# A transformer layer with attention and experts on one core: scores and maxima as pairs of 64-partition tiles, with a new order of TensorE's work

## The chip, the cores and the metric

The kernel runs on one core of a Trainium2 chip. The metric is the device time of one execution in microseconds (us), lower is better. TensorE's granted clock was 0.993 of full speed on average over the profiled execution.

## The reference

The input `x` holds 1024 tokens (a 32 x 32 image) of 384 channels. The layer is attention with decomposed relative positions, then a mixture of experts, each with a normalisation ahead and a residual behind:

```python
qkv = x @ w_qkv + b_qkv                      # 12 heads of 32 channels
attn = einsum('bnd,bmd->bnm', q * scale, k)  # 1024 x 1024 for each head
attn = attn + rel_h[..., :, None] + rel_w[..., None, :]   # rows r and columns w of the key's place
attn = softmax(attn); out = attn @ v
x = x + out @ w_proj + b_proj
# experts: top 2 of 8, 40 slots for each expert and group of 128 tokens, relu(t @ wi) @ wo, combined by the gates
```

`rel_h[q, r]` is the product of query q with a table row that depends on its own image row and on r; `rel_w[q, w]` likewise for image columns. All operands are 32-bit floats; the kernel splits the factors of its large products into a high and a low part of a rounded type (`fp32r`), and adds the products of the parts.

## The kernel before

The program is one list of instructions for each engine, written by hand, and semaphores are the only order between the lists. TensorE (PE) runs its list strictly in the order written. The stages are: load and normalise; project q and k (`qk`); relative terms (`rel_products`, `rel_turn`); values (`value_tile`, eight tiles of tokens, with max products between them); twelve heads of attention (`head`); projection; routing; experts. The change touches everything from the relative terms to the end of the heads.

For a head, one operand of 128 partitions holds all that a score needs. Query side `qst[b]` has 32 partitions of q, 32 of the low part of q (part 0) or of a row with the negated maximum (part 1), 32 of `rel_h` and 32 of `rel_w`. Key side `kst[b]` has k, k again or ones, and 64 constant rows (one-hot of the key's image row and column) that pick the relative terms. So a tile of 128 keys against 512 queries takes two matmuls of 128 x 128 x 512, and a score tile of 128 keys x 1024 queries takes four (`scores`, L597). `max_scores` (L584) makes the scores of 128 queries against 512 keys once more with one matmul, so that the largest of a row can be taken; there are 16 of them for a head (piece p). VectorE (DVE) takes the maximum of each piece (`reduce_max`, L1188), of all pieces (`whole_max`, L1192), TensorE turns the 128 x 8 result (`turn_max`, L589), DVE negates it (`negate_max`, L1198), and a small transfer puts it into `qst` (`max_row`, L340). The maxima run one head ahead: in `head(h)` TensorE makes pieces 5 to 15 for head h+1 and 0 to 4 for head h+2. Pieces use three PSUM banks in turn, so piece p waits until piece p-3 has been reduced.

ScalarE (ACT) takes the exponential of a score tile (L979) into one of six slots `prob`. GpSimd (POOL) adds seven of a head's eight tiles into `acc` (`add_probs`, L419 and L423), so that TensorE needs only the eighth tile and `acc` for the sum of a row. `values` multiplies each tile with the head's values as four column tiles of 32 (`quarters`, L606), two `prob` tiles for each i; with i = 3 it also does the sums (`ones` with `prob` and with `acc`). `pv_mm` then lets POOL begin the adds of the next head. `turn_output` (L630) turns the output and DVE normalises it.

The SyncE queue (SP) issues the transfers. `gather_head(h+2)` waits for the last score of head h-1 and then copies 32-partition strips inside SBUF into `qst` and `kst` in six transfers (1280 KB); it is needed by piece 0 of head h+2. Three buffers b = h mod 3 are used.

Of the kernel before, what the change touches and what calls it, by code (L numbers as in the profile page):

```python
# [5 lines left out]
ALU = mybir.AluOpType  # L6
# [13 lines left out]
def metaformer_layer(nc, x, w_qkv, b_qkv, w_proj, b_proj, rel_pos_h, rel_pos_w, w_router, wi, wo,  # L20
# [69 lines left out]
    attn = place("attn", [P, NT, D], F32, u1)  # L90
# [15 lines left out]
    rel = [new(n, [P, 2, DC, T], F32R) for n in ("relh", "relw")]  # L106
# [3 lines left out]
    onehot = place("onehot", [P, T], F32, v0 + 8 * BANK)  # L110

    q0, q1 = room(16 * T), room(16 * T)
    qst = [place(f"qst{b}", [P, 2, T], F32R, at_b) for b, at_b in enumerate((q0, q1, x0))]
    kst = [place(f"kst{b}", [P, 2, T], F32R, at_b + 8 * T) for b, at_b in enumerate((q0, q1, x0))]
# [9 lines left out]
    rhalf = new("rhalf", [P, NT, 2])  # L124
# [40 lines left out]
    with ctx:  # L165
# [8 lines left out]
        def wait(eng, s, value):  # L174
# [17 lines left out]
        xb_ready, k_rows, rows_set = sem("xb_ready"), sem("k_rows"), sem("rows_set")  # L192
# [4 lines left out]
        rel_products_mm, rel_copied, rel_mm, rel_act, rel_dve = (  # L197
            sem(n) for n in ("rel_products_mm", "rel_copied", "rel_mm", "rel_act", "rel_dve"))

        heads_in = [sem(f"heads_in{b}") for b in range(3)]  # L200
        vh_ready, max_mm, max_red, max_whole, max_turned, mneg_ready, mrow_in = (
            sem(n) for n in ("vh_ready", "max_mm", "max_red", "max_whole", "max_turned", "mneg_ready", "mrow_in"))
# [30 lines left out]
        HEAD_IN = 16 * 6  # L233
# [5 lines left out]
        REL = [(kind, c, half) for c in range(DC) for kind in range(2) for half in range(2)]  # L239
# [4 lines left out]
        PAIRS_T = NT // 2  # L244
        ADDED = 7
# [36 lines left out]

        def rel_views(part, n):


            kind, c, half = REL[n]
            b, w = bank(2 + n % 2), SIDE // 2
            if kind == 0:
                return rel[0][:, part, c, half * BANK:(half + 1) * BANK], b
            return (rel[1][:, part, c, :].rearrange("p (r w) -> p r w", w=SIDE)[:, :, half * w:(half + 1) * w],  # L290
                    b.rearrange("p (r w) -> p r w", w=w))
# [3 lines left out]
        def _(sp):  # L295
# [10 lines left out]
            sp.dma_start(onehot[2 * SIDE:4 * SIDE, :], onehot_c).then_inc(onehot_in, 16)  # L306
# [4 lines left out]
            def gather_head(h):  # L311
# [9 lines left out]
                if h in (1, 2):  # L321
                    sp.wait_ge(rows_set, 2)
                    sp.wait_ge(k_rows, 1)
                    for const, part in ((slice(2 * HD, 4 * HD), slice(0, 2)), (slice(HD, 2 * HD), slice(1, 2))):
                        sp.dma_start(kst[h][const, part, :].bitcast(F32), kst[0][const, part, :].bitcast(F32)).then_inc(rows_in[h - 1], 16)
                if h > 2:
                    sp.wait_ge(s_mm, 8 * (h - 2))
                both = [HD, 2, T]
# [6 lines left out]
                for dst, src in parts:  # L335
                    sp.dma_start(dst.bitcast(F32), src.bitcast(F32)).then_inc(heads_in[b], 16)  # L336

            def max_row(h):
                sp.wait_ge(mneg_ready, h + 1)
                sp.dma_start(qst[h % 3][HD:HD + 1, 1, :].rearrange("o (t q) -> o t q", q=P).bitcast(F32),  # L340
                             mneg[:, :].bitcast(F32)).then_inc(mrow_in, 16)
# [3 lines left out]
            gather_head(1)  # L345
            for h in range(NH):
                max_row(h)
                if h + 2 < NH:
                    gather_head(h + 2)
                if h == NH - 2:  # L350
                    sp.wait_ge(s_mm, 8 * (NH - 2))
                    sp.dma_start(wpj[:, :, :], w_proj.rearrange("(c p) n -> p c n", p=P)).then_inc(wpj_in, 16)
# [25 lines left out]
        def _(pool):  # L378
            nc.gpsimd.memset(ones[:, :], 1.0).then_inc(ones_set, 1)

            for i in range(2 * DC + 1):
# [8 lines left out]
                if i == 0:  # L390
# [4 lines left out]
            pool.wait_ge(onehot_in, 16)  # L395


            nc.gpsimd.memset(qst[0][HD:2 * HD, 1, :].bitcast(F32), 0.0).then_inc(rows_set, 1)
            nc.gpsimd.memset(kst[0][HD:2 * HD, 1, :].bitcast(F32), 1.0).then_inc(rows_set, 1)
            pool.wait_ge(rows_set, 2)  # L400
            nc.gpsimd.tensor_copy(kst[0][2 * SIDE:4 * SIDE, :, :],
                                  onehot[2 * SIDE:4 * SIDE, :].unsqueeze(1).broadcast_to([2 * SIDE, 2, T])).then_inc(k_rows, 1)
            pool.wait_ge(k_rows, 1)
            pool.wait_ge(ones_set, 1)
            pool.wait_ge(proj_mm, 4 * DC)
            nc.gpsimd.memset(qst[1][HD:2 * HD, 1, :].bitcast(F32), 0.0).then_inc(rows_set, 1)
            pool.wait_ge(rows_set, 3)
            pool.wait_ge(v_dve, NT)

            def head_values(h, b):  # L410

                wait(pool, pv_mm, PAIRS_T * (h - 2))
                nc.gpsimd.tensor_copy(vh[b][:, :, :], vt[:, :, bass.ts(h, HD)]).then_inc(vh_ready, 1)

            def add_probs(h, j, added=ADDED):

                pool.wait_ge(exp_done, NT * h + 2)
                wait(pool, pv_mm, PAIRS_T * h)
# [1031 lines left out]
```

## Time and profile before

| | us |
|---|---|
| median of 3 runs | 602.74 (600.71 to 602.84) |
| the profiled execution, its own time | 603.15 |
| its span, first to last instruction | 601.3 |
| relative terms 2nd and 3rd chunk, about 47.1 to 62.6 | 15.5 |
| value tiles, 62.6 to 77.4 | 14.8 |
| heads 0 to 11, 77.4 to about 276 | 199 |
| head 0, first exponential to that of head 1, 78.98 to 94.00 | 15.0 |
| one head in the middle | 16.52 |

The profile gives busy time by engine and by line. TensorE's busy time counts overlapping matmuls once. A matmul's duration is longer than the distance to the next, since they are pipelined: what a matmul costs is the distance between two starts. PEld are weight loads, which run under the matmul before.

### The profile page before, as it was taken

The numbers are of one execution on the slowest core, as the hardware profiler recorded it, in microseconds if no ns is written. First come the engines' busy times: TensorE is split into PE (matmuls) and PEld (weight loads), VectorE is DVE, ScalarE is ACT, GpSimd is POOL, SyncE is SP. The second block draws the span as 40 slices with busy tenths as digits, with TensorE's granted clock in tenths as the row PEclk, the third lists the DMA queues.
The fourth block names the chain that finished last, engine by engine and source line by source line (L and its number), as shares of the span: only waits on it lengthen the run. The fifth ranks groups of instructions, "written<-read, shape, count | busy, mean of one in ns | idle before, by whom it ended". The sixth has DMA issues, their size and how long they took to land.

```text
span 601.3 us, 11451 instructions
## 1 busy us (share of the span) xinstructions
PE 587.1 (98%) x4459; PEld 511.5 (85%) x4459; DVE 383.0 (64%) x643; ACT 295.2 (49%) x411; POOL 196.7 (33%) x115
## 2 busy tenths in 40 slices
PE   7999999999999999999989999999999999999996
PEld 7787977766677766668988999999999999999994
DVE  6646777777677776624888865554567555367525
ACT  4555245555555555563646444454545444455523
POOL 2300068889899888897000000000000000000000
PEclk9999999999999999999889999999999999999999
DMA  8046064444333334103412444443443434543202
GB/s 264 21 87 134 1 132 89 89 90 87 71 68 67 69 75 87 40 3 106 157 41 81 157 158 158 155 146 130 133 147 105 150 141 159 158 157 97 101 1 105
DMA packets 38615, 63.40 MB, mean 105 GB/s; under 512 B 3912, under 2 KB 34478, under 8 KB 38446
## 3 DMA queue, kind: packets, MB, share of 16 engines
q1 hardware_dynamic: 38574, 62.83, 37.0%
q8 instruction: 29, 0.48, 0.3%
q14 instruction: 12, 0.10, 0.0%
HBM read 44.16 MB, written 1.57 MB: 76 GB/s over the span
## 4 chain that ended last, share of the span: by engine, by line
PE 91%; DVE 3%; DMA 2%; ACT 1%; SPq 1%; issue 1%; DVEq 0%
PE ps L822 21%; PE ps L838 21%; PE ps L597 13%; PE ps L606 9%; PE ps L501 8%; PE ps L584 7%; PE ps L533 2%; PE ps L756 1%; PE ps L793 1%; PE ps L544 1%; PE ps L849 1%; PE ps L768 1%; SPq L336 1%; DMA kst<-kp 1%; PE ps L630 1%
## 5 line engine op out<-in xcount | busy, mean ns | idle before, releaser
L1188 DVE TENSOR_REDUCE rhalf<-ps 128x1 f32<-128x512 f32 x192 | 130.8, 690 | 33.6 <-PE ps L584 33.3
L423 POOL TENSOR_TENSOR acc<-acc,prob 128x1024 f32<-128x1024 f32 x58 | 139.7, 2408 | 8.7 <-ACT prob L979 4.0
L979 ACT ACTIVATE prob<-ps 128x1024 f32<-128x1024 f32 x96 | 98.1, 1028 | 80.7 <-PE ps L597 80.3
L597 PE MATMUL ps<-qst,kst 128*128 128x512 f32 x384 | 115.3, 396 | 0.5 <-DMA qst<-mneg 0.3
L451 POOL CAST dpc<-dpt 120x1024 fp32r<-120x1024 f32 (+1 forms) x3 | 3.1, 1042 | 274.8 <-PE ps L858 216.6
L822 PE MATMUL ps<-xeh,wih 128*128 128x320 f32 x288 | 89.6, 311 | 1.0 <-ACT xeh L1043 1.0
L838 PE MATMUL ps<-hh,woh 128*128 128x320 f32 x288 | 89.2, 310 | 0.0
L838 PE MATMUL ps<-hh,wol 128*128 128x320 f32 x288 | 89.0, 309 | 0.0
L822 PE MATMUL ps<-xeh,wil 128*128 128x320 f32 x288 | 89.0, 309 | 0.0
L838 PE MATMUL ps<-hl,woh 128*128 128x320 f32 x288 | 89.0, 309 | 0.0
L822 PE MATMUL ps<-xel,wih 128*128 128x320 f32 x288 | 89.0, 309 | 0.0
L597 PEld LDWEIGHTS ps<-qst,kst 128*128 128x128 f32 x384 | 70.1, 188 | 17.5 <-ACT prob L979 2.1
L584 PE MATMUL ps<-kst,qst 128*128 128x512 f32 x192 | 77.0, 407 | 1.4 <-DMA kst<-kp 0.8
L1276 DVE TENSOR_TENSOR wol<-raw_o,woh 128x1152 fp32r<-128x1152 f32 x32 | 43.4, 1357 | 50.8 <-ACT woh L1016 50.8
L1047 ACT ACTIVATE hh<-ps 128x320 fp32r<-128x320 f32 x96 | 41.8, 439 | 55.7 <-PE ps L822 55.1
L1016 ACT ACTIVATE woh<-raw_o 128x1152 fp32r<-128x1152 f32 x32 | 37.4, 1168 | 49.4 <-PE ps L838 49.4
L1271 DVE TENSOR_TENSOR wil<-raw_i,wih 128x1152 fp32r<-128x1152 f32 x32 | 43.4, 1357 | 24.4 <-ACT wih L1011 24.4
L1350 DVE SCALAR_TENSOR_TENSOR hl<-ps,hh 128x320 fp32r<-128x320 f32 x96 | 45.9, 488 | 20.0 <-ACT hh L1047 17.9
L822 PEld LDWEIGHTS ps<-xeh,wih 128*128 128x128 f32 x288 | 54.1, 188 | 1.2 <-ACT xeh L1043 1.2
L822 PEld LDWEIGHTS ps<-xel,wih 128*128 128x128 f32 x288 | 54.1, 188 | 0.0
L838 PEld LDWEIGHTS ps<-hl,woh 128*128 128x128 f32 x288 | 54.1, 188 | 0.0
L822 PEld LDWEIGHTS ps<-xeh,wil 128*128 128x128 f32 x288 | 54.1, 188 | 0.0
(162 smaller groups left out, 883.6 us busy)
## 6 DMA issues: line engine op xcount, KB each, us to landing
raw_i<-in_L_ffn_wi SPq DMA_DIRECT2D x32, 576.0 KB, 5.2
raw_o<-in_L_ffn_wo SPq DMA_DIRECT2D x32, 576.0 KB, 4.1
xs<-in_x SPq DMA_DIRECT2D x8, 384.0 KB, 4.7
qst<-qh SPq DMA_DIRECT2D x12, 256.0 KB, 3.1
qst<-relh SPq DMA_DIRECT2D x12, 256.0 KB, 3.9
qst<-relw SPq DMA_DIRECT2D x12, 256.0 KB, 4.4
kst<-kp SPq DMA_DIRECT2D x12, 256.0 KB, 5.1
qst<-ql SPq DMA_DIRECT2D x12, 128.0 KB, 3.0
```

The lines of the kernel that those rows point to most:

```text
L423: nc.gpsimd.tensor_tensor(acc[:, :], acc[:, :], prob[:, slot_of(j, t), :], ALU.add).then_inc(sum_add, 1)
L501: done = mm(out_bank, a, b, start=first and n == 0, stop=last and n == 2)
L584: mm(bank(max_bank(b, p)), qst[b][:, 0, t * P:(t + 1) * P], kst[b][:, 0, half * BANK:(half + 1) * BANK], start=True, stop=True).then_inc(m ...
L597: last = mm(bank(2 * (t % 2) + half), kst[b][:, part, t * P:(t + 1) * P], qst[b][:, part, half * BANK:(half + 1) * BANK], start=part == 0, ...
L606: last = mm(bank(6)[HD * j:HD * (j + 1), cols], stationary, moving[:, j * Q4:(j + 1) * Q4], start=start, stop=stop, skip_group_check=True)
L822: last = mm(bank(k, SLOTS), w[:, b, c, k * P:(k + 1) * P], xe[:, c, e, :], start=c == 0 and n == 0, stop=c == DC - 1 and n == 2)
L838: last = mm(bank(3 + c, SLOTS), w[:, b, k, c * P:(c + 1) * P], h[:, b, k, :], start=s == 0 and k == 0 and n == 0, stop=s == UNITS - 1 and ...
L979: run(prob[:, slot_of(j, t), :], ps[:, 2 * (t % 2) * BANK:2 * (t % 2 + 1) * BANK], ACT.Exp).then_inc(exp_done, 1)
L1188: ve.tensor_reduce(rhalf[:, p // 2, p % 2:p % 2 + 1], bank(max_bank(b, p)), AX_X, ALU.max).then_inc(max_red, 1)
L1271: ve.tensor_tensor(wil[:, b, :, :], raw_i[:, b, :, :], wih[:, b, :, :].bitcast(F32), ALU.subtract).then_inc(wi_lo, 1)
L1276: ve.tensor_tensor(wol[:, b, :, :], raw_o[:, b, :, :], woh[:, b, :, :].bitcast(F32), ALU.subtract).then_inc(wo_lo, 1)
L1350: stt(out=hl[:, b, k, :], in0=bank(k, SLOTS), scalar=0.0, in1=hh[:, b, k, :].bitcast(F32), op0=ALU.max, op1=ALU.subtract).then_inc(h_lo, 1)
```

## The change

The scores are cut differently. An operand now has two halves of 64 partitions, one for each half of the queries (`side`), each with 32 partitions of q or k and 32 of something else: `qm[b]` has four slots of 512 queries (slot 0: low part of q with `rel_w` low and the maximum; slot 1: high part of q with `rel_w` high; slots 2 and 3: high part of q with the two halves of `rel_h`), and `km[b]` two. Every matmul uses 64 partitions. The two sides stand one behind the other in the list, on different rows of the array and into different banks. A score tile takes six matmuls (three pairs) where it took four; a head's maxima take 16 as before, in eight pairs.

The maxima no longer contain `rel_h`: DVE reduces each piece over image columns only, to 16 numbers for a partition (128x16 where it was 128x1), keeps 128 x 256 of them, adds `rel_h` (`relhn`, one 128x256 add) and takes the maximum of 32 for each tile. `rel_w` is shifted by its last column first, so that one constant row is free for the maximum (`rel_shift`, a copy of 16 columns on ACT and a 128x512 subtraction on DVE in six of the twelve steps of the relative terms).

`gather_head` issues twelve transfers instead of six, in two groups with a semaphore each (`max_in`: k, q high and `rel_w`; `rest_in`: the rest). POOL's memsets of `qst` are gone; the constant rows come from memory by eight small transfers and two POOL copies.

TensorE's list for a head is new: behind each score tile stands one pair of max pieces and at most one other thing. The first eight pieces for head 1 are made between the value tiles 4 to 7. Sums are steps of their own (`sum_tiles`, `sum_added`), behind score tile 2. DVE's list puts `normalise` behind piece 15, and `negate_max` behind the first two reductions of the head after; its loop over heads is unrolled.

```diff
-                parts = [(qst[b][0:HD, :, :], qh[rows, chunk, :].unsqueeze(1).broadcast_to(both)),
-                         (qst[b][HD:2 * HD, 0, :], ql[rows, chunk, :]),
-                         (qst[b][2 * HD:3 * HD, :, :], rel[0][rows, :, chunk, :]),
-                         (qst[b][3 * HD:4 * HD, :, :], rel[1][rows, :, chunk, :]),
-                         (kst[b][0:HD, :, :], kp[rows, :, chunk, :]),
-                         (kst[b][HD:2 * HD, 0, :], kp[rows, 0, chunk, :])]
+                first, rest = [], []
+                for side in range(2):
+                    low, cols = side * P // 2, slice(side * BANK, (side + 1) * BANK)
+                    own, near = slice(low, low + HD), slice(low + HD, low + 2 * HD)
+                    first += [(km[b][own, :, :], kp[rows, :, chunk, :]),
+                              (qm[b][own, HIGH:4, :], qh[rows, chunk, cols].unsqueeze(1).broadcast_to([HD, 3, BANK])),
+                              (qm[b][near, LOW:HIGH + 1, :], relw[rows, chunk, side, :, :])]
+                    rest.append((qm[b][own, LOW, :], ql[rows, chunk, cols]))
+                    for v in range(2):
+                        kh = slice(rows.start + v * HALF_ROWS, rows.start + (v + 1) * HALF_ROWS)
+                        rest.append((qm[b][near, 2 + v, :], relh[kh, :, chunk, cols]))
...
-                t, half = p // 2, p % 2
-                mm(bank(max_bank(b, p)), qst[b][:, 0, t * P:(t + 1) * P], kst[b][:, 0, half * BANK:(half + 1) * BANK],
-                   start=True, stop=True).then_inc(max_mm, 1)
+                t, half, side = p // 4, p // 2 % 2, p % 2
+                rows = slice(side * P // 2, (side + 1) * P // 2)
+                mm(bank(max_bank(b, p)), qm[b][rows, HIGH, t * P:(t + 1) * P],
+                   km[b][rows, 0, half * BANK:(half + 1) * BANK], start=True, stop=True).then_inc(max_mm, 1)
...
+                units = [(HIGH, 0), (2 + t // HALF, 1), (LOW, 0)]
+                for k, (q_slot, k_slot) in enumerate(units):
+                    if k == 2 and t == 0:
                         pe.wait_ge(mrow_in, 16 * (h + 1))
+                    for side in range(2):
+                        rows = slice(side * P // 2, (side + 1) * P // 2)
+                        last = mm(bank(2 * (t % 2) + side), km[b][rows, k_slot, t * P:(t + 1) * P],
+                                  qm[b][rows, q_slot, :], start=k == 0, stop=k == 2)
+                last.then_inc(s_mm, 1)
...
+                scores(h, n, b, 0)
+                if first:
+                    pe.wait_ge(v_dve, NT)
+                next_max(4)
+                former_values(2)
+                scores(h, n, b, 1)
+                next_max(5)
+                former_values(3)
+                scores(h, n, b, 2)
+                next_max(6)
+                if not first:
+                    sum_tiles(h - 1, (b - 1) % 3, range(ADDED, NT))
+                    sum_added(h - 1)
...
+                scores(h, n, b, 3)
+                next_max(7)
+                if not first:
+                    turn_output(h - 1)
+                scores(h, n, b, 4)
+                after_max(0)
+                scores(h, n, b, 5)
...
+                values(h, b, 0)
+                if not last:
+                    turn_max(h + 1, (b + 1) % 3)
+                after_max(1)
+                scores(h, n, b, 6)
+                values(h, b, 1)
+                after_max(2)
+                scores(h, n, b, 7)
+                after_max(3)
...
+                if t >= HALF:
+                    for p in range(2 * (t - HALF), 2 * (t - HALF + 1)):
+                        max_scores(1, 0, 1, p)
...
+                ve.tensor_tensor(rhalf[:, :, :], rhalf[:, :, :],
+                                 relhn[:, h // HPG, :, h % HPG * SIDE:(h % HPG + 1) * SIDE], ALU.add).then_inc(max_sum, 1)
+                dve.wait_ge(max_sum, h + 1)
                 ve.tensor_reduce(rmax[:, :], rhalf[:, :, :], AX_X, ALU.max).then_inc(max_whole, 1)
```

The end of head 0 on TensorE, from the values behind score tile 5 on, before the change (L606 are `values`, L589 is `turn_max`, L584 a max piece, L597 scores):

```order
L606 MATMUL ps<-prob,vh_100 32x256 x16
L589 MATMUL ps<-ident,rmax 8x128
L584 MATMUL ps<-kst_94,qst_91 128x512
L597 MATMUL ps<-qst_89,kst_92 128x512 x2
L584 MATMUL ps<-kst_94,qst_91 128x512
L597 MATMUL ps<-qst_89,kst_92 128x512 x2
```

The same place in the changed kernel (L639 values, L617 `turn_max`, L612 a pair of max pieces, L631 three pairs of scores):

```order
L631 MATMUL ps<-qm_90,km_93 128x512 x6
L639 MATMUL ps<-prob,vh_101 32x256 x8
L617 MATMUL ps<-ident,rmax 8x128
L612 MATMUL ps<-km_95,qm_92 128x512 x2
L631 MATMUL ps<-qm_90,km_93 128x512 x6
L639 MATMUL ps<-prob,vh_101 32x256 x8
L612 MATMUL ps<-km_95,qm_92 128x512 x2
L631 MATMUL ps<-qm_90,km_93 128x512 x6
L612 MATMUL ps<-km_95,qm_92 128x512 x2
```

The values of a head now stand in single steps between score tiles, and the pair behind `turn_max` is the one with piece 2, which waits for the negated maximum; before, that piece came later behind several scores.

DVE's list from the first head's maxima on, before the change (L1188 `reduce_max`, L1192 `whole_max`, L1198 `negate_max`):

```order
L1188 TENSOR_REDUCE rhalf<-ps 128x1 x16
L1192 TENSOR_REDUCE rmax<-rhalf 128x8
L1198 TENSOR_SCALAR mneg<-ps 8x128
L1188 TENSOR_REDUCE rhalf<-ps 128x1 x5
```

And in the changed kernel (L1257 reductions, L1264 the added sum, L1267 `whole_max`, L1273 `negate_max`, L1279 and L1281 `normalise`):

```order
L1257 TENSOR_REDUCE rhalf<-ps 128x16 x14
L1279 RECIPROCAL rl<-ps 128x8
L1281 TENSOR_TENSOR attn<-ps,rl 128x2x4x32
L1264 TENSOR_TENSOR rhalf<-rhalf,relhn 128x256
L1267 TENSOR_REDUCE rmax<-rhalf 128x8
L1257 TENSOR_REDUCE rhalf<-ps 128x16 x2
L1273 TENSOR_SCALAR mneg<-ps 8x128
```

Between the last reduction and the negation there now stand the normalisation, the add, a longer reduction and two reductions for the next head.

## Rows read from the trace of the kernel before

**Rows 1.** The page: busy time of each engine, share, instructions.

```profile
PE 587.1 (98%) x4459; PEld 511.5 (85%) x4459; DVE 383.0 (64%) x643; ACT 295.2 (49%) x411; POOL 196.7 (33%) x115
```

**Rows 2.** Windows: busy time by engine, of one middle head.

```profile
core 0: us, PE busy (x) PEld busy (x) DVE busy (x) ACT busy (x) POOL busy (x), PEclk, DMA share, GB/s
143.30:159.80 16.50, 16.50 (x135) 11.57 (x133) 11.99 (x20) 8.81 (x9) 14.69 (x8) 1.00 0.39 80
```

**Rows 3.** Groups by line in one head, 143.3 to 159.82.

```profile
L423 POOL TENSOR_TENSOR acc<-acc,prob 128x1024 f32<-128x1024 f32 x6 | 14.4, 2394 | 0.8 <-ACT prob L979 0.4
L1188 DVE TENSOR_REDUCE rhalf<-ps 128x1 f32<-128x512 f32 x16 | 11.1, 691 | 3.2 <-PE ps L584 3.2
...
L597 PEld LDWEIGHTS ps<-qst,kst 128*128 128x128 f32 x32 | 5.9, 188 | 1.3 <-ACT prob L979 0.2
```

**Rows 4.** Timeline of PE: start, us, instruction, count.

```profile
243.75 0.39 PE L584 MATMUL ps<-kst,qst 128*128 128x512 f32 x1
244.06 1.93 PE L606 MATMUL ps<-prob,vh 128*32 128x256 f32 x32
245.82 0.61 PE L606 MATMUL ps<-prob,ones 128*32 128x256 f32 x8
246.25 0.61 PE L606 MATMUL ps<-acc,ones 128*32 128x256 f32 x8
246.79 0.50 PE L584 MATMUL ps<-kst,qst 128*128 128x512 f32 x1
247.13 0.62 PE L597 MATMUL ps<-qst,kst 128*128 128x512 f32 x2
247.59 0.40 PE L584 MATMUL ps<-kst,qst 128*128 128x512 f32 x1
...
249.88 0.60 PE L630 MATMUL ps<-ident,osb 128*128 128x128 f32 x4
250.23 1.18 PE L597 MATMUL ps<-qst,kst 128*128 128x512 f32 x4
```

**Rows 5.** Timeline of POOL over one head.

```profile
147.85 2.41 POOL L419 TENSOR_TENSOR acc<-prob 128x1024 f32<-128x1024 f32 x1 [1.05 <-PE ps L606]
150.70 12.28 POOL L423 TENSOR_TENSOR acc<-acc,prob 128x1024 f32<-128x1024 f32 x5 [0.44 <-ACT prob L979]
...
164.37 2.41 POOL L419 TENSOR_TENSOR acc<-prob 128x1024 f32<-128x1024 f32 x1 [1.05 <-PE ps L606]
```

**Rows 6.** Timeline of DVE in one head.

```profile
151.57 0.20 DVE L1204 RECIPROCAL rl<-ps 128x8 f32<-128x8 f32 x1
151.91 0.42 DVE L1206 TENSOR_TENSOR attn<-ps,rl 128x256 f32 x1
...
154.67 0.17 DVE L1192 TENSOR_REDUCE rmax<-rhalf 128x8 f32<-128x16 f32 x1
156.01 0.28 DVE L1198 TENSOR_SCALAR mneg<-ps 8x128 fp32r<-8x128 f32 x1 [1.17 <-PE ps L589]
```

**Rows 7.** DMA, 158 to 170 in 40 slices: one gather.

```profile
DMA  0000000999999999999989999999200000000000
DMA packets 416, 1.31 MB, mean 109 GB/s; under 512 B 96, under 2 KB 96, under 8 KB 416
```

**Rows 8.** Timeline of PE between the value tiles and head 0.

```profile
77.22 0.33 PE L501 MATMUL ps<-wvh,xnl 128*128 128x384 f32 x1
77.40 0.39 PE L584 MATMUL ps<-kst,qst 128*128 128x512 f32 x1
```

**Rows 9.** Timeline from the sums of head 10 to those of head 11.

```profile
262.05 1.14 POOL L438 CAST wph<-wpj 128x1152 fp32r<-128x1152 f32 x1
262.38 0.61 PE L606 MATMUL ps<-acc,ones 128*32 128x256 f32 x8
...
265.72 8.39 POOL L423 TENSOR_TENSOR acc<-acc,prob 128x1024 f32<-128x1024 f32 x3
...
275.48 0.61 PE L606 MATMUL ps<-acc,ones 128*32 128x256 f32 x8
```

More of the change, by code:

```diff
@@ L105, in metaformer_layer @@
     ath, atl = place("ath", [P, DC, T], F32R, k0), place("atl", [P, DC, T], F32R, k0 + TD)
-    rel = [new(n, [P, 2, DC, T], F32R) for n in ("relh", "relw")]
+    relh = new("relh", [P, 2, DC, T], F32R)
+    relw = new("relw", [P, DC, 2, 2, BANK], F32R)
     v0 = room(TD)
@@ L237, in metaformer_layer @@
         WARM = 22
-        REL = [(kind, c, half) for c in range(DC) for kind in range(2) for half in range(2)]
+        REL = [(kind, c, half) for c in range(DC) for kind in (1, 0) for half in range(2)]
         V_BANKS = [0, 1, 2, 6]
@@ L321, in gather_head @@
                 if h in (1, 2):
[L322 to L325, printed above, removed]
+                    sp.wait_ge(k_rows, 2)
+                    for low in (0, P // 2):
+                        const = slice(low + HD, low + 2 * HD)
+                        sp.dma_start(km[h][const, :, :].bitcast(F32), km[0][const, :, :].bitcast(F32)).then_inc(rows_in[h - 1], 16)
@@ L527, in rel_products @@
                 kind, c, half = REL[n]
-                wait(pe, rel_copied, n - 1)
+                if n > 1:
+                    pe.wait_ge(*rel_left(n - 2))
                 for t in range(HALF):
@@ new lines, in next_max, with after_max, former_values @@
+                def next_max(k):
+                    if not last:
+                        for p in (2 * k, 2 * k + 1):
+                            max_scores(*nxt, p)
+                def after_max(k):
+                    if more and not last:
+                        if first and k == 0:
+                            pe.wait_ge(rows_in[1], 32)
+                        for p in (2 * k, 2 * k + 1):
+                            max_scores(*after, p)
+                def former_values(i):
+                    if not first:
+                        values(h - 1, (b - 1) % 3, i)
@@ new lines, in head @@
+                scores(h, n, b, 3)
+                next_max(7)
+                if not first:
+                    turn_output(h - 1)
+                scores(h, n, b, 4)
+                after_max(0)
+                scores(h, n, b, 5)
+                if last:
+                    turn_attn(1)
+                values(h, b, 0)
+                if not last:
+                    turn_max(h + 1, (b + 1) % 3)
+                after_max(1)
+                scores(h, n, b, 6)
+                values(h, b, 1)
@@ L969, in free_slot @@
                 then, was = (h, t - SLOT) if t >= SLOT else (h - 1, t + NT - SLOT)
-                if was % 2 == 0:
-                    wait(act, pv_mm, PAIRS_T * then + was // 2 + 1)
+                if was >= ADDED:
+                    wait(act, pv_mm, PV_STEPS * (then + 1))
+                elif was % 2 == 0:
+                    wait(act, pv_mm, PV_STEPS * then + was // 2 + 1)
                 if was < ADDED:
@@ L1241, in _ @@
                     negate_max(0, 0)
+                if t >= HALF:
+                    reduce_max(1, 1, 2 * (t - HALF))
+                    reduce_max(1, 1, 2 * (t - HALF) + 1)
             head(0, 0, first=True)
-            with dve.Fori(0, (NH - 3) // 3) as i:
-                for j in range(1, 4):
-                    head(3 * i + j, j % 3)
+            for h in range(1, NH - 2):
+                head(h, h % 3)
             head(NH - 2, (NH - 2) % 3, more=False)
```

266 lines of the change are left out of this document (133 added, 133 removed).

## The prediction

> **What bounds the kernel now.** I read the page first: TensorE is busy for 98% of the span [rows 1], and the heads are a third of the time. A window over one middle head has TensorE busy for all of its 16.5 us, at full clock (2.4 GHz, granted clock 1.00), while DVE works 12.0, ACT 8.8 and POOL 14.7 [rows 2]. So TensorE's list sets the pace, and POOL stands close behind. The timeline of POOL gives the length of a head: its first add starts at 147.85 and again at 164.37, 16.52 apart [rows 5].
>
> What fills the 16.52 follows from distances between starts. In rows 4 two score matmuls take 247.13 to 247.59, 0.23 each (I use 0.229); 32 small matmuls of the values take 244.06 to 245.82, so a group of four column tiles costs 0.22 (I use 0.217). Between the starts at 243.75 and 247.13 lie 3.38 us; two 512-column matmuls and 12 groups explain 3.05, and 0.33 is left for going to column tiles and back. That is the price of one excursion [rows 4]. A head has 48 large matmuls (32 scores, 16 maxima) 10.99, 20 groups 4.34, the turned output 0.43 (249.88 to 250.23 and 0.08 until the matmuls are in step again), two excursions 0.66, and about 0.15 of waits for exponentials: 16.57, which closes on 16.52.
>
> POOL's own loop is the next bound. Its adds are 2.39 to 2.41 long and 2.47 apart (five fill 12.28 [rows 5]); 0.44 of the loop is a wait for the third exponential. Without that wait it runs 2.41+0.07+12.28 = 14.76; then come TensorE's two groups with `acc`, 0.61 [rows 4], and about 0.15 and 0.18 for the semaphores there and back: 15.70. No head can be shorter, however fast TensorE gets.
>
> **The change part by part.**
>
> *Fewer matmul slots.* A head goes from 48 single matmuls to 32 pairs. No row shows two row tiles at once. The nearest one is the four column tiles, whose matmuls start together and cost 0.217 a group, not four times that [rows 4]; so I take a pair as one slot plus the 0.007 by which such tiles start apart: 0.236. The bounds are 0.229 and, if the two run after one another, 0.458. Weight loads: one takes 188 ns [rows 3], less than a slot, and four turned 128x128 tiles, each with a load of 128 columns, pass in 0.35 to 0.43 [rows 4], about 0.1 each; so even two loads in a row fit into a slot of 0.236, barely. 32 x 0.236 = 7.55 instead of 10.99: 3.4 saved.
>
> *More changes of tile shape.* Values and sums no longer stand together: V2, V3, sums, V0 (with `turn_max`) and V1 are five excursions from the 64-row shape to column tiles, and `turn_output`, which cost none before, is a sixth. At 0.33 each this is 1.98 instead of 0.66. The work of a head becomes 7.55+4.34+0.43+1.98 = 14.3. The Trainium skill speaks against the change here (TensorEngine Tiling, Key Properties: changing the tiling mode drains TensorE). The 0.33 of rows 4 agrees and is what I use; without the rule the sum is the same.
>
> *New waits for DVE.* A piece waits for the reduction three pieces before. A reduction is 0.69 [rows 3], two of them 1.38. The third pair stands behind V1, the fourth behind score tile 7, the fifth behind score tile 0 of the next head; from one to the next are 3+1 slots, 0.94, so DVE falls 0.44 behind twice; with about 0.2 in hand, 0.67 of wait. Piece 1 of the head after needs the last but one reduction of the head's maxima: 0.17. The third wait is the largest. Behind piece 15 DVE now has 0.23+0.43 (normalise [rows 6]), the new add, the longer reduction, two reductions 1.38 and the negation 0.28. Neither add nor reduction over 256 numbers is in the trace; a 128x256 op takes 0.42, a reduction of 16 numbers 0.17 [rows 6] and of 512 0.69 [rows 3], on the line between them 256 give 0.42; bounds 0.17 and 0.69; I take 0.42 and 0.07 to the next for each. That sums to 3.4 us, while TensorE meanwhile has score tile 5, V0 and `turn_max`, 2.2. The pair behind it has piece 2, which needs the negated maximum: 1.2 us in which everything behind it on TensorE stands. Before, five pieces were placed so late that this was free (DVE waited 1.17 for the turn, not TensorE [rows 6]). Waits: 2.0; a head takes 14.3+2.0 = 16.3, 0.23 less than before. With ten such heads (1 to 10): **-2.3**.
>
> *Gather.* 1.31 MB flow from about 160.1 to 166.6, 202 GB/s [rows 7]. The first group is 1.18 MB, lands about 7.5 us after the last score of head h-1, and is needed at about 9.7: hidden by score tiles 0 to 4, 2 us to spare. Were it late, each us would cost a us. The second group (0.39 MB) has a whole head. Head 0 is different: `gather_head(2)` starts only when the last value tile is done and has 0.52 MB of constant rows ahead, so 1.70 MB need 1.3+8.4+0.3 = 10.0 us, but head 0 reaches piece 0 of head 2 after five score tiles and four pairs, some 6 us (4.5 of matmuls; DVE's eight reductions 5.5). Then 5.8 follow. Head 0 takes 15.8 instead of 15.0: **+0.8**, although eight maxima left it.
>
> *Value tiles.* TensorE's list is gapless here too, from value matmuls (0.17 to 0.18 apart) straight into a max piece [rows 8]; two pieces behind a tile cost two slots, 0.46. Now each pair costs 0.24 and an excursion of its own, 0.56. Tiles 0 to 3: +0.4. Tiles 4 to 7 had nothing: +2.2. `turn_max` behind tile 4 waits for the add and the longer reduction, +0.6. Together **+3.2**.
>
> *Relative terms.* In steps with `rel_w` the path from product to turn has a small copy and a 128x512 subtraction on DVE (0.69, as the reduction of 512 [rows 3]) where one copy on ACT was; the next step's products cover most, and the first max piece now waits less for k. I take **+0.3**, bounds -0.6 and +2. The small loads at the start delay `wv` by a few us, and it is needed only for the value tiles at 62.6.
>
> *The end.* Head 11 has no maxima. From the `acc` sum of head 10 to that of head 11 went 13.1 [rows 9]. TensorE now is free earlier, but POOL's `wph` copy and five tiles end at 274.1 [rows 9], 12.0 after its last add, and the sum waits for them: -1.0; as head 10 has fewer maxima, TensorE catches up with POOL there, -0.3. **-1.3**.
>
> Sum: -2.3+0.8+3.2+0.3-1.3 = +0.7, on the profiled 603.15: 603.85. The median of the runs is 0.41 lower, so I forecast **603.4**.
>
> **Rivals.**
>
> *TensorE's waits vanish and POOL's loop is the bound (faster).* For it: POOL has only 0.6 between its 15.70 and my 16.3; if excursions are cheaper or DVE's chain shorter, the wait behind `turn_max` shrinks. It decides when work plus waits fall under 15.7. Ten heads at 15.70 give -8.2 instead of -2.3: 597.5. Chance 0.31.
>
> *A pair costs more than a slot, or the excursion into row tiles does (slower).* Nothing in the trace shows two row tiles, and two weight loads fill a slot nearly to the end. Each 0.01 on the pair is 0.32 a head of work, partly eaten by the waits. At a slot of 0.30 the work is 16.3 and about 1.0 of waits stay: 17.3, ten heads +10, with head 11 and the rest +2: 616. At 0.1 more for each change of shape, 17.1: 612. It decides from a pair of 0.25 on. The Trainium skill (TensorE: Matmul & The Clock Gate, Measured speedup vs the span model) has four row tiles of 512 columns at 3.07 times instead of four; that would be a slot of 0.30, this rival. Chance 0.25.
>
> *The pairs do not overlap at all.* 64 slots of 0.229 and 14.3-7.55 of the rest: 21.4 without waits, +4.9 a head, with head 11, 0 and the value tiles 660. Against it stand the column tiles [rows 4]. Chance 0.06.
>
> **How the numbers follow.** Forecast 0.38. A measurement of this kernel tells about 0.5% (3.0 us) from no change; 599.7 to 605.8 is "same". The forecast's own range, from its unknown costs (0.17 to 0.69 for DVE's two, relative terms, excursions), is 600 to 606.5; some of it is slower, some faster: same 0.35, faster 0.33 (the POOL rival and a little of the forecast), slower 0.32. The range takes in the first rival down to 596.5 and the second up to 615.
>
> **What would show it.** A head of 16.3 between POOL's first adds; starts of score pairs 0.236 apart with both sides within 0.01; a hole of about 1.2 us on TensorE ahead of the third and fourth max piece, ended by the negation; about 0.33 around each step of values; head 0 with a wait for the gather; POOL waiting about 0.5 more for TensorE than in its own loop. Wrong, if the starts of score pairs are further apart, if POOL never waits for the sums, or if the gather ends waits in the middle heads.

## The result and the profile after

| | before | changed |
|---|---|---|
| median of the runs | 602.79 us (600.71 to 603.17) | 629.26 us (627.79 to 631.42) |
| ratio | | 1.0444, 95% interval 1.0416 to 1.0473 |
| profiled span | 601.3 us | 629.6 us |
| mean granted clock of TensorE | 0.993 | 0.963 |
| first exponential of head 0 | 78.98 | 81.74 |
| head 0 | 15.01 | 19.17 |
| heads 1 to 10, mean | 16.45 | 18.50 |
| end of the last exponential | 273.57 | 301.89 |

A head is counted here from its first exponential to that of the next. The rows from the profiled span on are of the profiled executions (603.15 and 631.42 us). The last exponential ends 28.3 us later, as the whole span does: everything is lost before the projection, and heads 1 to 10 lose 20.5 us of it.

The page of the changed kernel, the line that answers to [rows 1], and the group of the maxima (busy, mean ns of one, idle before, releaser):

```profile
PE 588.6 (93%) x4651; PEld 484.1 (77%) x4651; DVE 405.0 (64%) x661; ACT 292.0 (46%) x411; POOL 193.5 (31%) x112
...
L612 PE MATMUL ps<-km,qm 64*128 64x512 f32 x192 | 53.4, 474 | 16.5 <-DVE mneg L1273 11.5
```

TensorE's share fell from 98% to 93%. Of its idle time 16.5 us stand ahead of the max pairs, and DVE's negation ended 11.5 of them. Two middle heads as windows, against [rows 2], and a stretch of head 0 (the column after POOL is the granted clock):

```profile
core 0: us, PE busy (x) PEld busy (x) DVE busy (x) ACT busy (x) POOL busy (x), PEclk, DMA share, GB/s
213.80:231.20 17.40, 15.10 (x151) 8.70 (x149) 13.18 (x22) 8.70 (x9) 14.35 (x7) 1.00 0.44 86
137.40:157.70 20.30, 18.00 (x151) 10.15 (x150) 13.60 (x22) 8.70 (x9) 15.92 (x8) 0.83 0.39 79
88.40:91.60 3.20, 0.00 (x0) 0.00 (x0) 1.33 (x2) 0.00 (x0) 2.97 (x2) 0.50 0.92 176
```

Even at full clock a head takes 17.4 us, with 2.3 of them idle. The other head has the same 151 matmuls and the same 2.3 us idle, and takes 2.9 more at a mean clock of 0.83. The clock was below 1.00 in six of heads 1 to 10. Where the 2.3 us stand is in TensorE's timeline (in brackets the idle time ahead and what ended it), which answers to [rows 4]:

```profile
215.61 0.40 PE L612 MATMUL ps<-km,qm 64*128 64x512 f32 x2
215.94 1.07 PE L639 MATMUL ps<-prob,vh 128*32 128x256 f32 x16
216.94 0.96 PE L631 MATMUL ps<-qm,km 64*128 64x512 f32 x6
...
219.07 0.96 PE L631 MATMUL ps<-qm,km 64*128 64x512 f32 x6
219.87 0.40 PE L612 MATMUL ps<-km,qm 64*128 64x512 f32 x2
220.19 0.66 PE L664 MATMUL ps<-ident,osb 128*128 128x128 f32 x4
220.78 0.97 PE L631 MATMUL ps<-qm,km 64*128 64x512 f32 x6
221.59 0.54 PE L612 MATMUL ps<-km,qm 64*128 64x512 f32 x2
221.82 1.01 PE L631 MATMUL ps<-qm,km 64*128 64x512 f32 x6
222.76 1.07 PE L639 MATMUL ps<-prob,vh 128*32 128x256 f32 x16
224.89 0.27 PE L617 MATMUL ps<-ident,rmax 128*8 128x128 f32 x1 [1.06 <-DVE rmax L1267]
226.40 0.58 PE L612 MATMUL ps<-km,qm 64*128 64x512 f32 x2 [1.24 <-DVE mneg L1273]
```

DVE and POOL in the same head, against [rows 5, 6]:

```profile
221.73 0.42 DVE L1281 TENSOR_TENSOR attn<-ps,rl 128x256 f32<-128x256 f32 x1
222.19 2.19 DVE L1264 TENSOR_TENSOR rhalf<-rhalf,relhn 128x256 f32<-128x256 f32 x1
224.42 0.42 DVE L1267 TENSOR_REDUCE rmax<-rhalf 128x8 f32<-128x256 f32 x1
224.87 1.29 DVE L1257 TENSOR_REDUCE rhalf<-ps 128x16 f32<-128x512 f32 x2
226.08 0.27 DVE L1273 TENSOR_SCALAR mneg<-ps 8x128 fp32r<-8x128 f32 x1
...
219.25 2.39 POOL L445 TENSOR_TENSOR acc<-prob 128x1024 f32<-128x1024 f32 x1 [2.72 <-PE ps L639]
221.72 9.79 POOL L449 TENSOR_TENSOR acc<-acc,prob 128x1024 f32<-128x1024 f32 x4
```

This is the point of the whole case. The new add takes 2.19 us. It starts at 222.19, 0.47 after a POOL add began (221.72), and ends at 224.38, 0.28 after that one must be over (four fill 9.79, so 2.4 each). The operation of the same size just ahead, `attn<-ps,rl`, has one operand in PSUM and takes 0.42 under a POOL add too; in the kernel before it took 0.42 from 151.91 on, when a POOL add had run for 1.2 us [rows 5, 6]. Of all twelve relative adds, one is short:

```profile
L1264 DVE TENSOR_TENSOR rhalf<-rhalf,relhn x12: 424/2190/2319, 72.8 to 279.1; 128x256 f32<-128x256 f32 x12
```

(shortest, median, longest in ns): the short one is for the maxima of head 0, made at 72.8 ahead of the heads, when POOL adds nothing. The time of head 0 itself was lost in another way, at the gather of head 2:

```profile
85.41 1.18 PE L631 MATMUL ps<-qm,km 64*128 64x512 f32 x6
91.64 0.79 PE L612 MATMUL ps<-km,qm 64*128 64x512 f32 x2 [5.04 <-DMA qm<-relw]
92.20 1.51 PE L631 MATMUL ps<-qm,km 64*128 64x512 f32 x6
93.64 1.82 PE L639 MATMUL ps<-prob,vh 128*32 128x256 f32 x16
```

After 5.04 us of waiting the value matmuls take 1.82 us in place of 1.07: the clock stood at 0.50 from 88.4 to 93.3.

### The profile page after: what moved, and what is told of

It is laid out like the page before. It is cut to its first block, busy times and chain, and to the rows that moved or that the text cites. A ratio compares the mean times of both kernels' runs of the same rounds, so it can differ in the third digit from the quotient of the medians.

```text
span 629.6 us, 11786 instructions
## 1 busy us (share of the span) xinstructions
PE 588.6 (93%) x4651; PEld 484.1 (77%) x4651; DVE 405.0 (64%) x661; ACT 292.0 (46%) x411; POOL 193.5 (31%) x112
## 4 chain that ended last, share of the span: by engine, by line
PE 82%; DVE 10%; POOL 2%; issue 2%; ACT 1%; SPq 1%; DMA 1%; DVEq 0%; POOLq 0%
PE ps L868 20%; PE ps L884 20%; PE ps L631 9%; PE ps L639 8%; PE ps L524 8%; PE ps L612 5%; DVE rhalf L1264 3%; DVE rhalf L1257 3%; POOL acc L449 2%; PE ps L557 1%; PE ps L802 1%; PE ps L489 1%; PE ps L506 1%; PE ps L839 1%; PE ps L895 1%
## 5 line engine op out<-in xcount | busy, mean ns | idle before, releaser
L1257 DVE TENSOR_REDUCE rhalf<-ps 128x16 f32<-128x512 f32 x192 | 121.9, 685 | 53.9 <-PE ps L612 53.3
L631 PE MATMUL ps<-qm,km 64*128 64x512 f32 x576 | 96.7, 431 | 0.1
L631 PEld LDWEIGHTS ps<-qm,km 64*128 64x128 f32 x576 | 57.3, 199 | 22.6 <-issue 8.9
L612 PE MATMUL ps<-km,qm 64*128 64x512 f32 x192 | 53.4, 474 | 16.5 <-DVE mneg L1273 11.5
L639 PE MATMUL ps<-prob,vh 128*32 128x256 f32 x768 | 56.7, 417 | 0.0
```

The lines of the kernel that those rows point to most:

```text
L612: mm(bank(max_bank(b, p)), qm[b][rows, HIGH, t * P:(t + 1) * P], km[b][rows, 0, half * BANK:(half + 1) * BANK], start=True, stop=True).the ...
L631: last = mm(bank(2 * (t % 2) + side), km[b][rows, k_slot, t * P:(t + 1) * P], qm[b][rows, q_slot, :], start=k == 0, stop=k == 2)
L639: last = mm(bank(6)[HD * j:HD * (j + 1), cols], stationary, moving[:, j * Q4:(j + 1) * Q4], start=start, stop=stop, skip_group_check=True)
L1257: ve.tensor_reduce(rhalf[:, t, half * HALF_ROWS:(half + 1) * HALF_ROWS], bank(max_bank(b, p)).rearrange("p (r w) -> p r w", w=SIDE), AX_X, ...
```

## Experiments

Theory: DVE's add, both operands in SBUF, waits for the whole POOL instruction in progress; TensorE waits behind it twice a head; with these holes its clock falls. Rivals: the added work on DVE counts by itself, the two engines share bandwidth, the pairs or their changes of shape are dear, the low clock comes from elsewhere.

The time is the median of the runs; the heads are those of the profiled execution.

| kernel | us | ratio to before (interval) | head 0 | heads 1 to 10 |
|---|---|---|---|---|
| changed | 629.3 | 1.0444 (1.0416 to 1.0473) | 19.2 | 18.50 |
| a1, without the add | 603.6 | 1.0025 (1.0006 to 1.0044) | 18.8 | 15.53 |
| a2, POOL's adds in halves | 615.7 | 1.0225 (1.0199 to 1.0250) | 19.5 | 16.54 |
| a3, before with a spare add | 609.1 | 1.0103 (1.0069 to 1.0137) | 14.9 | 16.91 |
| a4, sides apart in the list | 628.3 | one run | 19.7 | 18.27 |
| b1, add done by POOL | 610.5 | 1.0136 (1.0109 to 1.0164) | 19.0 | 16.12 |
| b2, reordered | 601.6 | 0.9976 (0.9963 to 0.9988) | 18.7 | 15.47 |
| b3, holes filled | 622.2 | 1.0310 (1.0282 to 1.0338) | 22.4 | 17.60 |
| b4, head 0 mended | 623.1 | 1.0348 (1.0316 to 1.0381) | 15.5 | 17.88 |
| c1, score pairs in one row tile | 669.5 | one run | 25.8 | 19.9 at full clock |
| b5, b2 with head 0 and head 10 mended | 596.4 | 0.9901 (0.9880 to 0.9922) | 16.8 | 15.46 |

**a1.** The add is left out, so the maximum lacks `rel_h`.

```diff
-                ve.tensor_tensor(rhalf[:, :, :], rhalf[:, :, :],
-                                 relhn[:, h // HPG, :, h % HPG * SIDE:(h % HPG + 1) * SIDE], ALU.add).then_inc(max_sum, 1)
-                dve.wait_ge(max_sum, h + 1)
```

> The changed kernel without the 128x256 add of relh in whole_max (the maximum lacks rel_h, so the exponentials are shifted by another number; everything else is computed). Theory 1, the add on DVE has to wait for a running POOL add (2.19 us instead of 0.42) and TensorE waits for DVE, by which its clock falls too: the heads go from 18.5 to about 16.2 us, the clock in them to 1.00 but for head 0, and the whole to about 606 us. Rival, the stalls and the low clock come from the six changes of tile shape and the other waits, and the add only adds its own length: heads about 18, the whole about 622 us.

603.6 us: one operation is worth 25.7 us, 2.97 a head, seven times its own 0.42. At 15.53 the heads are even shorter than the bound of 15.70 in my prediction, and the clock is 1.00 from 99.36 to 254.70.

**a2.** Each of POOL's adds becomes two of 512 columns.

```diff
+                for n in range(2):
+                    cols = slice(n * BANK, (n + 1) * BANK)
+                    src = acc[:, cols] if first is None else prob[:, slot_of(j, first), cols]
+                    last = nc.gpsimd.tensor_tensor(acc[:, cols], src, prob[:, slot_of(j, t), cols], ALU.add)
```

> The changed kernel with each POOL add of 1024 columns made as two of 512. If an instruction holds the path that DVE's two-input add needs until it ends, the add now waits for the rest of a 1.2 us instruction only: it takes 0.5 to 1.6 us instead of 2.19, heads get up to 1 us shorter and the whole comes to 612 to 622 us, although POOL pays about 0.4 us a head for six more instructions. Rival, the two engines share the path at half speed each: the add keeps about 2.2 us and the whole is 629 to 634 us.

The timeline of a2, DVE's add and POOL's beside it:

```profile
194.51 1.24 DVE L1271 TENSOR_TENSOR rhalf<-rhalf,relhn 128x256 f32<-128x256 f32 x1
...
194.19 6.65 POOL L445 TENSOR_TENSOR acc<-acc,prob 128x512 f32<-128x512 f32 x5
```

POOL does the same adds in pieces half as long, and DVE's add falls to 1.24 us. The wait goes by POOL's instruction, not by its load; sharing of bandwidth falls. The hole ahead of the turn is nearly gone (0.6 us in all), and the one ahead of the next max pair stays at 1.2 us a head. With this one hole the granted clock is 1.00 from 102.13 to 267.50, so that a head takes 1.96 us less, where I had expected up to 1. By the Trainium skill (SBUF — State Buffer, SBUF: two separate sides) the port pair of the two engines is an exclusive lock for a whole instruction, and DVE needs it when it has two SBUF inputs. The trace agrees: 2.19, 1.24 with halves, and 0.42 for `attn<-ps,rl`.

**a3.** The kernel before, with a spare 128x256 add in SBUF ahead of its whole maximum.

```diff
+                ve.tensor_tensor(spare[:, :], spare[:, :], spare[:, :], ALU.add).then_inc(spare_done, 1)
```

> The kernel before with one more DVE add of 128x256, both inputs in SBUF, on spare zeros, between the last reduction and whole_max of each head. Theory 1: it takes up to 2.2 us there too when a POOL add runs, turn_max comes late, TensorE stands about 1 us a head and perhaps loses clock: 612 to 625 us. Rival, the length of 2.19 belongs to the operands and their layout in the changed kernel, or the old order hides it: the add takes 0.42 or the time stays 603 to 606 us.

The spare add takes about 1.16 us in the heads and 0.42 ahead of them, and a head grows by 0.46, 4.6 us for ten. The time, 609.1, lies between both expectations, since only the part of the wait that nothing covers counts; in the profiled execution another 2.8 us were lost ahead of the heads, where the clock was 0.83 in the first 20 us. So the add waits in the old kernel too, but the older order covers more than half: the wait is not a matter of the new tiles, its price is one of place.

**a4.** The six matmuls of a score tile, side after side.

```diff
-                for k, (q_slot, k_slot) in enumerate(units):
-                    for side in range(2):
+                for side in range(2):
+                    for k, (q_slot, k_slot) in enumerate(units):
```

> The changed kernel with the six matmuls of a score tile ordered side after side, so that neighbours use the same rows of the array and cannot run together. If the pairs work, 24 slots of 0.229 come back in each head, 5.5 us, of which the waits hide 0.5 to 1.5: about 680 us. Rival, the pairs bring little because the head is bound by waits: below 650 us.

```profile
209.69 0.94 PE L631 MATMUL ps<-qm,km 64*128 64x512 f32 x6
210.55 1.07 PE L639 MATMUL ps<-prob,vh 128*32 128x256 f32 x16
```

Six matmuls pass in 0.86 us, as in the changed kernel: both sides still run side by side, though three of one stand ahead of three of the other. The edit left the pairing in force, so its 628.3 us say nothing on what pairs are worth, though they lie in the rival's range; c1 does.

**b1.** POOL does the relative add, behind its first add of a head (its loop is written out for this).

```diff
+                if h < NH - 1:
+                    m = h + 1
+                    pool.wait_ge(max_red, 2 * NT * (m + 1))
+                    nc.gpsimd.tensor_tensor(rhalf[:, :, :], rhalf[:, :, :],
+                                            relhn[:, m // HPG, :, m % HPG * SIDE:(m % HPG + 1) * SIDE], ALU.add).then_inc(max_sum, 1)
```

> The changed kernel with the 128x256 relative add of heads 1 to 11 done by POOL, right behind the first of its own adds of a head, in place of DVE. Nothing is left out. Theory (the add was late because DVE with both operands in SBUF waits for the POOL instruction in progress): on POOL it waits for nobody, the maximum is turned at once, the two TensorE waits behind L617 and L612 (1.06 and 1.24 us a head) go, heads 1 to 10 take 15.6 to 15.9 us and the time is 603 to 608 us. Rival (the step between the last reduction and the turn is long in itself, or POOL, with six adds of 2.39, a copy of 0.39 and now this add, becomes the bound): heads of 16.5 us or more, 613 to 622 us.

Both happened in part, and 610.5 us lies between the two ranges. The wait ahead of `turn_max` is gone, the one for the negation fell from 1.24 to about 0.5 a head, and POOL is the bound, in its timeline:

```profile
187.30 2.39 POOL L445 TENSOR_TENSOR acc<-prob 128x1024 f32<-128x1024 f32 x1 [0.53 <-PE ps L643]
189.65 0.73 POOL L449 TENSOR_TENSOR rhalf<-rhalf,relhn 128x256 f32<-128x256 f32 x1
190.34 12.47 POOL L454 TENSOR_TENSOR acc<-acc,prob 128x1024 f32<-128x1024 f32 x5
202.75 0.40 POOL L439 COPY vh<-vt 128x256 f32<-128x256 f32 x1
203.68 2.39 POOL L445 TENSOR_TENSOR acc<-prob 128x1024 f32<-128x1024 f32 x1 [0.53 <-PE ps L643]
```

One loop is 16.38 us with the 0.73 of the add in it; TensorE now waits for `acc` ten times, 6.4 us in all, 3.4 of them for head 10's.

**b2.** The add stays on DVE; what stands around it moves. Maxima get a second buffer, the banks are numbered anew (piece 4 waits for the negation, not piece 2).

```diff
                 values(h, b, 0)
-                if not last:
-                    turn_max(h + 1, (b + 1) % 3)
                 after_max(1)
                 scores(h, n, b, 6)
+                if not last:
+                    turn_max(h + 1, (b + 1) % 3)
...
+                if more:
+                    for p in range(2):
+                        reduce_max(h + 2, after, p)
                 whole_max(h + 1)
                 if more:
-                    for p in range(2):
-                        dve.wait_ge(max_whole, h + 2)
+                    for p in range(2, 4):
                         reduce_max(h + 2, after, p)
                 negate_max(h + 1, nxt)
```

> The changed kernel with the add left on DVE, but out of the way: a second buffer for the half-row maxima lets DVE reduce tiles 0 to 3 of the head after around the add, and TensorE turns the maximum behind score tile 6 in place of ahead of it (tile 4 of the head after now waits for the negation, in place of tile 2). Nothing is left out. Theory (the 2.19 us of the add matter only because TensorE stands behind them): the add stays about 2.2 us long, the waits behind L617 and L612 go, heads take 15.5 to 15.8 us, 603 to 607 us. Rival (the delay only moves on, to the maximum's row of the next head or to the reductions): heads stay over 16.8 us, 613 to 625 us.

```profile
203.05 0.98 DVE L1265 TENSOR_TENSOR rhalf<-rhalf,relhn 128x256 f32<-128x256 f32 x1
...
198.90 2.39 POOL L447 TENSOR_TENSOR acc<-prob 128x1024 f32<-128x1024 f32 x1 [0.47 <-PE ps L640]
201.37 12.31 POOL L451 TENSOR_TENSOR acc<-acc,prob 128x1024 f32<-128x1024 f32 x5
```

Heads of 15.47 us and 27.6 us off the changed kernel, a little below the range. TensorE no longer waits for the maximum in a middle head. One part of the expectation missed: the add takes 0.98, since it now starts 1.7 us into a POOL add (203.05 after 201.37) and not 0.5. So the reorder took away the place and part of the length at once.

**b3.** Five spare 128x512 matmuls ahead of the turn and five behind it, in the two holes.

```diff
+                    for _ in range(5):
+                        mm(bank(max_bank(b, NP)), km[b][:, 1, 0:P], km[b][:, 0, 0:BANK], start=True, stop=True)
                 pe.wait_ge(max_whole, h + 1)
```

> The changed kernel with five spare 128x512 matmuls ahead of each turn of a maximum and five behind it, into banks that are free then (1.2 us each five, about the two waits of 1.06 and 1.24 us). Nothing is left out. Theory (the granted clock falls because TensorE stands idle twice in a head): the waits stay in length but are filled, the clock holds at 1.00 through the heads, heads take 17.4 to 17.9 us and the time is 617 to 622 us. Rival (the low stretches come from elsewhere, or the fillers delay more than they save): 627 to 635 us.

The add is as long as before (2.19), and TensorE does useless work where it waited; the granted clock from 103.6 to 279.6 us is 1.00, and a head takes 17.60 instead of 18.50. This splits the loss of heads 1 to 10 against a1: 20.7 us (17.60 less 15.53, ten times) are the waits, 9.0 the clock of the changed kernel's profiled execution. The fillers made head 0 3.2 us longer, which is why the total gained 7.1 only.

**b4.** Pieces 0 to 7 of head 2 stand behind score tiles 6 and 7 of head 0.

```diff
-                after_max(0)
+                if not first:
+                    after_max(0)
                 scores(h, n, b, 5)
...
                 scores(h, n, b, 6)
+                if first:
+                    after_max(0)
                 values(h, b, 1)
-                after_max(2)
+                after_max(1 if first else 2)
                 scores(h, n, b, 7)
+                if first:
+                    after_max(2)
                 after_max(3)
```

> The changed kernel with the eight maximum tiles of head 2 that stand in head 0 put behind its score tiles 6 and 7 in place of 4 to 7. Nothing is left out. Theory (head 0 lost its 4.2 us to the wait of 5.04 us for the gather of head 2 and to the low clock behind it): that wait shrinks below 1 us, head 0 takes 15 to 16.5 us, 622 to 626 us. Rival (the four pairs bunch up before DVE, which needs 1.4 us for each, or head 1 is then late): no gain, 628 to 631 us.

Head 0 fell from 19.2 to 15.5, 3.7 us, and the wait for the gather is gone; the median gained 6.2. Heads 1 to 10 hold the same two holes, and 17.88 in the table is no gain of the edit: in this profiled execution (619.0, the fastest of four) the clock was below 1.00 in three of them, in the changed kernel's in six.

**c1.** From b2: both matmuls of a score pair take the partitions of side 0, so side 1 of each score tile is computed from side 0's queries.

```diff
-                        rows = slice(side * P // 2, (side + 1) * P // 2)
+                        rows = slice(0, P // 2)
```

> The reordered kernel (b2, heads of 15.47 us), but both matmuls of every score pair take their operands from the same 64 partitions, those of side 0, so that they can't lie in different row tiles. It changes the computation: side 1 of each score tile is computed from side 0's queries. Theory (the pairs do run at once and a pair costs one slot of 0.236): now the 24 score pairs of a head take two slots, 24 x 0.23 = 5.5 us more, heads of 20.6 to 21.4 us, and over 12 heads about 64 us: 655 to 675 us. Rival (two matmuls in different row tiles are no faster than two in the same, as the earlier run with the sides apart left open): heads under 17 us, 600 to 620 us.

The time lies in its range by luck: a stretch of low clock (last section) made head 1 34.2 us long, 14 more than the heads behind it. Windows of it and of full clock:

```profile
101.00:141.00 40.00, 40.00 (x172) 23.52 (x165) 15.03 (x23) 8.93 (x10) 17.12 (x9) 0.51 0.20 40
180.00:200.00 20.00, 19.96 (x150) 12.53 (x149) 13.49 (x22) 8.79 (x9) 14.72 (x8) 1.00 0.40 79
```

In the second window TensorE is all but never idle, and a head takes 19.9, a little under the range. Four score matmuls of one tile in a row:

```profile
213.10 1.07 PE L632 MATMUL ps<-qm,km 64*128 64x512 f32 x4
```

One lasts 0.39, so they start 0.227 apart. A head of 19.9 less 24 second slots of 0.227 leaves 14.5 us, TensorE's own work in a head of the changed kernel. So two matmuls in different row tiles cost one slot, and two in the same tile cost two.

**b5.** b2, b4's edit, and one tile of head 10's sum given to TensorE (POOL adds one fewer).

```diff
-            add_probs(NH - 2, (NH - 2) % 3)
+            add_probs(NH - 2, (NH - 2) % 3, ADDED - 1)
...
-                    sum_tiles(h - 1, (b - 1) % 3, range(ADDED, NT))
+                    sum_tiles(h - 1, (b - 1) % 3, range(ADDED - last, NT))
```

> The reordered kernel (b2), with the eight maximum tiles of head 2 put behind score tiles 6 and 7 of head 0 (b4's edit), and one tile of head 10's sum taken from POOL and given to TensorE. Nothing is left out. Theory: head 0 goes from 18.7 to about 15.5 us (-3.2), the wait of 2.1 us for the sum of head 10 goes and the low clock behind it at 272.7 with it (-2 to -3), heads 1 to 10 stay at 15.5: 595 to 598 us, faster than the kernel before by 0.8 to 1.3%. Rival (the two waits cover other late work that then shows: the tables of the projection, DVE's reductions of head 2): 599 to 602 us, no more than b2's.

596.4 us, in the range, 1.0% faster than the kernel before and 5.2% faster than the changed one. Head 0 came to 16.8, not 15.5 (a hole of 1.6 us stayed in it); the last exponential ends at 268.20, 4.7 before b2's.

## Why the prediction was wrong

The forecast was 603.4; the time is 629.3, outside the range. By its terms, in us, as the two profiled executions have them (28.3 apart; the medians are 26.5 apart):

| term | forecast | measured |
|---|---|---|
| heads 1 to 10 | -2.3 | +20.5 |
| head 0 | +0.8 | +4.2 |
| value tiles and relative terms | +3.5 | +2.8 |
| the end | -1.3 | +0.9 in head 11, nothing behind it |

**The step that failed** is the price of DVE's new add: "Neither add nor reduction over 256 numbers is in the trace; [...] bounds 0.17 and 0.69; I take 0.42". The reduction took 0.42 exactly, and so did the add while POOL was idle. Under POOL's adds it took 2.19, three times my upper bound, and TensorE stood behind it. The nearest row [rows 6] was an add of the same size, but with one operand in PSUM; I matched the size and not where the operands lie. The trace of before did hold a warning. In [rows 9] three POOL adds take 8.39 us, more than three times 2.39 [rows 3], and it is the last one that is long; beside it DVE subtracted weights, both operands in SBUF:

```profile
270.51 1.35 DVE L1258 TENSOR_TENSOR wpl<-wpj,wph 128x1152 fp32r<-128x1152 f32 x1
270.79 3.33 POOL L423 TENSOR_TENSOR acc<-acc,prob 128x1024 f32<-128x1024 f32 x1
```

Here POOL came second, and its add took 0.9 longer. I used that row for its end only. a1, a2, a3 and b2 show this cause. None of the three signs that I had named as "wrong" appeared; the term that failed had no sign of its own.

**The size of the waits.** The chain behind the last reduction was forecast at 3.4 us (its terms add up to 3.3) and its wait at 1.2. It took 4.8 (221.50 to 226.35): the add 1.77 more than forecast, the rest less, as two reductions take 1.21 and not 1.38. TensorE had 2.6 of work meanwhile, not 2.2, and the wait became 2.3 (1.06 and 1.24). The mechanism, a hole ahead of the pair that needs the negation, was right. At full clock a head came to 17.4 for my 16.3; what is neither TensorE's own 14.5 nor the 2.3 is 0.6; I had 0.84 of small waits for reductions.

**The clock had no term.** For the one hole of 1.2 us that I forecast it needed none: a2 has just this hole in each head, holds 1.00 and takes 16.54 a head, near my 16.3. The clock fell with two holes, of 2.3 us in all, and b3 prices that at 9.0 us in ten heads. The price differs between executions: b4's heads 1 to 10, with the same two holes, are only 2.8 us longer than b3's.

**TensorE's work was right.** 14.3 forecast, 14.5 by c1; the pair's start behind a pair is 0.23 (221.59 to 221.82). An excursion to the columns and back is 0.33: from 215.61 to 216.94 lie a pair and four groups of value matmuls (1.10), 0.23 is left, and the first pair behind takes 0.10 more. For the turned output it is 0.35: from 219.07 to 221.59 lie seven pairs (1.65), the turned output 0.43, and 0.44 is left, of which 0.09 still belongs to the columns ahead of 219.07. So the rival of dear pairs, 612 to 616, is not what happened, though its side was right. The Trainium skill's figure beside it (TensorE: Matmul & The Clock Gate, Measured speedup vs the span model) is for four row tiles, which no run here has; between two pairs at full clock a slot of 0.30 appears nowhere.

**The POOL rival** was right as a bound and 0.13 too high: 15.70 forecast; b2's POOL loop turns in 15.57, a1's head in 15.53. It was reached only with DVE's add left out or out of TensorE's way. That a1 (603.6) and b2 (601.6) come out beside my forecast is luck: their heads 1 to 10 are 9.2 and 9.8 us shorter than before, not 2.3, and heads 0 and 11 take back 8.9 and 7.0. In b2 the six adds take 14.78 (198.90 to 213.68; forecast 14.76), and the two groups with their semaphores 0.79 in place of 0.94.

**Head 0.** The gather ended 9.9 us after the head's first exponential, as forecast (10.0). Behind it I had 5.8 us and there were 9.3, with the clock near 0.5 until 95.4. DVE's add has little part in it: a1, without the add, has 9.05 there (90.31 to 99.36). b4 shows that nearly all of it hung on the wait: head 0 took 15.5, with the add as slow as before (2.17).

**Value tiles.** With full clock in the first 20 us (a1, b1 to b4) the first exponential comes at 80.6 to 81.3, so the term is +1.6 to +2.3 where I had +3.5; no run here took it apart. **The end** was +0.9 and not -1.3: TensorE waited 1.23 us for head 10's `acc`, which it did not in the kernel before. With faster heads POOL is further behind, 2.85 us in a1; b5 removed that.

## What to carry to other kernels

Price an operation by a row whose operands lie in the same memories, next to the same neighbours, not by its shape alone; a DVE operation with two SBUF inputs beside a POOL that is hardly ever idle can cost nearly one POOL instruction more (here 2.19 us for 0.42, beside adds of 2.39). Where such a wait can't be avoided, put other matmuls between it and the one that needs its result: the same add cost 3 us a head in one order and nothing in another. A forecast that creates holes on TensorE must ask what they do to its clock: one hole of 1.2 us a head cost it nothing (a2), two cost 9.0 us in ten heads (b3). One that shortens a stage needs the next bound, here POOL at 15.57.

## What the runs showed of the hardware

- Matmuls in different row tiles run at once even when three of one tile stand in the list ahead of the other's (a4: six in 0.86 us). The Trainium skill (TensorEngine Tiling (Array Packing), Key Properties) says that tiles operate independently; the trace agrees, here even for tiles that are not neighbours in the list.
- A DVE add with two inputs in SBUF that starts while a POOL add runs ends 0.28 to 0.29 us behind that POOL add: so it is in all 44 such adds of the changed kernel, a2, a3 and b2. It takes 2.19 us when it starts 0.47 into a POOL add of 2.38, 1.24 when 0.33 into one of 1.29 (a2), 1.16 when 1.50 into one of 2.38 (a3), 0.98 when 1.68 into one (b2), and 0.43 when 2.21 into one, in b2's head 0.
- The granted clock fell in six of the ten middle heads of the changed kernel and in three of b4's. They have two holes each, of 1.06 and 1.24 us, with only the turn (0.27) between them, and at full clock TensorE is busy for 15.1 us of 17.4. With the holes filled (b3, 103.6 to 279.6), or with only the second one (a2, 102.13 to 267.50), it was 1.00 throughout.
- Once down, the clock can stay down in a full list: in c1 it was 0.51 from 101 to 141 us with TensorE busy for 40.00 of 40 us, one head took 34.2 us, and it was 1.00 again behind. In head 0 of the changed kernel, after a hole of 5.04 us, it was at 1.00 again from 95.4 on. The cause is open.
- With both inputs in SBUF the 128x256 add takes 0.73 us on POOL, and 0.42 on DVE while POOL is idle.
